# A decoder layer on one core: the bias of the attention's values moves from VectorE's add to a product of TensorE, and ScalarE copies the values out

## The chip, the cores and the metric

The kernel runs on one core of a Trainium2 chip. A core has five engines that run at the same time, each through its own list of instructions in order: TensorE (PE in the profile; its weight loads are PEld), VectorE (DVE), ScalarE (ACT), GpSimd (POOL) and SyncE (SP, which issues most DMAs). They wait for each other through semaphores. The metric is device time in microseconds, a median over runs. Matrix products are written into PSUM, a memory of a few banks that TensorE fills and VectorE or ScalarE reads.

## The reference, cut to what matters

The layer is a Mamba block, a cross attention with a feed-forward part, and a mixture of 160 experts, each with a residual and a layer norm. There are 8 batches of 256 positions, 256 channels wide. The change concerns the line of V:

```
# cross attention; keys = values = ctx, 256 positions a batch
Q = queries @ Wq + bq
K = keys @ Wk + bk
V = values @ Wv + bv
scores = einsum('bqd,bkd->bqk', Q, K) * scale
attn = einsum('bqk,bkd->bqd', softmax(scores), V)
merged = attn @ Wo + bo
x = layer_norm(queries + keys + values + merged, ln1_g, ln1_b)
h = relu(x @ W1 + b1) @ W2 + b2
x = layer_norm(x + h, ln2_g, ln2_b)
# around it: x = layernorm(x + mamba(x)); x = layernorm(x + above); x = layernorm(x + experts(x))
```

## The kernel before, in words

The program has three parts on the time axis: a front (Mamba, attention, feed-forward, router; to about 690 us and a tail to about 765), the experts, and a final combine. The change is in the front.

The front is a software pipeline over the 8 batches. It runs in turns; in turn s the engines work on the state scan of batch s, the attention of batch s-1, the feed-forward of batch s-2, the router of batch s-3 and the projections of batches s+1 and s+2. Each engine has a function `turn(s, p)` that writes out by hand in which order it takes these pieces, so the order on an engine is fixed; p is the parity that picks one of two buffers. An instruction that waits holds up all that its engine has behind it.

The scan of a batch has 16 steps t (4 groups of states for each of 4 chunks of channels). A step goes through four engines: ScalarE writes the decays into a PSUM tile DA (`decay`, L722 and L725: a small copy and four exponentials); GpSimd forms the inflow product (`inflow`, L462); VectorE runs the scan (`scan`, L1662) and multiplies it (`outflow`, L1669); TensorE sums it into the bank Y (`sum_`, L1117). After each four steps VectorE takes the sum out of Y (`y`, L1675 and L1678), and the next first sum of TensorE waits for that.

The keys and values of batch s are made in turn s. TensorE projects the keys into the bank PB (`k_`, L1197), ScalarE copies them out with their bias (L745), TensorE projects the values into the same bank (`v_`, L1206, four products), and VectorE adds the bias row on the way out to the tile vv (`v_`, L1684), between the scan and the outflow of step 12. PB is used next by the projection of batch s+2 (`in_proj`, L1081), which waits for the semaphore v_c that this add raises. Before the first turn that uses them, the weight of V and its row are multiplied by the output projection, so that the row `rows[:, BV, :]` holds the products' bias, the same on all 128 partitions.

The last steps of the feed-forward of batch s-2 stand near by. VectorE adds the residual and takes the moments (`ln2`, L1723, L1688, L1692). GpSimd makes the root (`ln_root`, L468 to L473), then adds an offset for another batch (`x1_offset`, L508). ScalarE normalises (`normalise`, L769), GpSimd multiplies by the norm's weights (`ln2_affine`, L503), and VectorE adds the residual (`ln3`, L1729). On GpSimd, behind L503, follow two scatters of the routed rows of batch s-3 (L515), two more roots, the inflow products of steps 14 and 15 and of the next turn's 0 and 1, the other norm's affine (L491, L493), two scatters, and the product of step 2. On VectorE, in the next turn, the router of batch s-3 forms a mask (`choose`, L1759) behind the outflow of step 0.

On ScalarE the order around the change is: the keys' copy L745, decay 12, decay 13, the normalise L769 of batch s-2, the copy of the projection (`x_in`, L659), decay 14.

Of the kernel before, what the change touches and what calls it, by code (L numbers as in the profile page):

```python
# [11 lines left out]
ALU = mybir.AluOpType  # L12
AX = mybir.AxisListType

P = 128
NB, T, D = 8, 256, 256
NT = NB * T
KD = D // P
QT = T // P
# [61 lines left out]
def decoder_kernel(nc, a, out):  # L81
    ctx = ExitStack()
    with ctx:
        def sb(name, shape, dt=FP32):
            return ctx.enter_context(nc.sbuf_tensor(name, shape, dt))

        def ps(name, shape=(P, 512), dt=FP32):
            return ctx.enter_context(nc.psum_tensor(name, list(shape), dt))

        def sig(name, per=1):  # L90
            return Sig(ctx.enter_context(nc.semaphore(name)), per)
# [22 lines left out]
        w_v = sb("w_v", [P, KD, D])  # L114
# [6 lines left out]
        rows = sb("rows", [P, 7, D])  # L121
        BV, BO, G1, B1, B2, G2, BB2 = range(7)
# [4 lines left out]
        ident = sb("ident", [P, P])  # L127
# [16 lines left out]
        PB = ps("PB")  # L144
# [34 lines left out]
        v_f, v_c, kT_f, kT_c = sig("v_f"), sig("v_c"), sig("kT_f"), sig("kT_c")  # L179
# [4 lines left out]
        vo_f, vo_c = sig("vo_f", 2), sig("vo_c", 2)  # L184
# [29 lines left out]
        ct = sb("ct", [P, KD, T])  # L214
# [19 lines left out]
        vv = sb("vv", [P, QT, D])  # L234
# [43 lines left out]
        def pair(bank):  # L278
            return bank[:, :].rearrange("p (c t) -> p c t", c=2)

        def states(tile):
            return tile[:, :].rearrange("p (n t) -> p n t", n=SG)
# [3 lines left out]
        def exists(b):  # L286
            return not isinstance(b, int) or 0 <= b < NB
# [362 lines left out]
        def front_scalar(act):  # L650
            s = nc.scalar
# [18 lines left out]
            def z_in(b, p, f):  # L670
                if f == 0 and y_d.at(b - 2, NC, True):
                    act.wait_ge(y_d.sem, y_d.at(b - 2, NC))
                act.wait_ge(proj_f.sem, proj_f.at(b, f + 5))
                s.activation(sz[p][:, 2 * f:2 * f + 2, :], pair(PB), ACT.Copy).then_inc(proj_c.sem, 1)
# [38 lines left out]
            def decay(b, p, t):  # L713
                gr, c = t % NG, t // NG
                if t == 0:
                    act.wait_ge(dl_d.sem, dl_d.at(b, 1))
                    if isinstance(b, int) and b == 0:
                        act.wait_ge(k_scaled.sem, 2)
                if outflow_d.at(b, t - NDA + 1, True):
                    act.wait_ge(outflow_d.sem, outflow_d.at(b, t - NDA + 1))  # L720
                da = states(DA[t % NDA])
                s.activation(da[:, :, 0:1], zeros[:, 0:SG].unsqueeze(2), ACT.Copy)  # L722
                for n in range(SG):
                    st = gr * SG + n
                    ins = s.activation(da[:, n, 1:T], dl[p][:, c, 1:T], ACT.Exp, scale=a_neg[:, c, st:st + 1])  # L725
                ins.then_inc(decay_d.sem, 1)
# [74 lines left out]
            for c in range(NC):  # L801
                for k in range(TAPS):
                    ins = s.activation(w_tap[:, c * TAPS + k, :], ident[:, :], ACT.Copy, scale=w_conv[:, c, k:k + 1])
# [35 lines left out]
            def turn(s, p):  # L839
                if exists(s) and s > 0:  # L840
                    decay(s, p, 1)
                    decay(s, p, 2)
                if exists(s + 1) and s >= 0:
                    conv_out(s + 1, 1 - p, 1)
                if exists(s) and s > 0:
                    decay(s, p, 3)
                if exists(s + 1) and s >= 0:
                    z_in(s + 1, 1 - p, 0)
                if exists(s):
                    decay(s, p, 4)  # L850
                if 0 <= s < 3:
                    clear_near(s)
                if exists(s):
                    decay(s, p, 5)
                if exists(s - 2):
                    copy_out(s - 2, x2aT_f, QF, fT, x2aT_c)
                if exists(s - 3):
                    chosen_exp(s - 3)
                if exists(s + 1) and s >= 0:
                    z_in(s + 1, 1 - p, 1)  # L860
                    gates(s + 1, 1 - p)
                if exists(s - 2):
                    ffn1(s - 2, 0)
                if exists(s):
                    decay(s, p, 6)
                if exists(s + 1) and s >= 0:
                    x_proj(s + 1, 1 - p)
                if exists(s - 2):
                    ffn1(s - 2, 1)
                if exists(s):  # L870
                    decay(s, p, 7)
                if s == 0:
                    turned_out()
                if exists(s - 1):
                    normalise(s - 1, 0, x1[1 - p])
                if exists(s - 2):
                    ffn1(s - 2, 2)
                if exists(s - 1):
                    copy_out(s - 1, x1T_f, QA, aT, x1T_c)
                if exists(s):  # L880
                    decay(s, p, 8)
                if s == 2:
                    clear_rest()
                if exists(s + 1) and s >= 0:
                    dt_proj(s + 1, 1 - p, 0)
                if exists(s - 1):
                    q_(s - 1)
                if exists(s - 2):
                    ffn1(s - 2, 3)
                if exists(s):  # L890
                    decay(s, p, 9)
                if s == 0:
                    vo_out()
                if exists(s):
                    decay(s, p, 10)
                if exists(s + 1) and s >= 0:
                    dt_proj(s + 1, 1 - p, 1)
                    softplus(s + 1, 1 - p)
                if exists(s - 1):
                    softmax(s - 1)  # L900
                if exists(s):
                    decay(s, p, 11)
                if exists(s + 1) and s >= 0:
                    softplus_ln(s + 1, 1 - p)
                if exists(s - 1):
                    copy_out(s - 1, pT_f, QA, qT, pT_c)
                if exists(s):
                    k_(s)
                    decay(s, p, 12)
                    decay(s, p, 13)  # L910
                if exists(s - 2):
                    normalise(s - 2, 2, x2[p])
                if exists(s + 2) and s > -2:
                    x_in(s + 2, 0)
                if s == -1:
                    decay(0, 0, 2)
                if exists(s):
                    decay(s, p, 14)
                if exists(s - 2):
                    normalise(s - 2, 3, x2[p])  # L920
                if exists(s + 2) and s > -2:
                    x_in(s + 2, 1)
                if s == -1:
                    decay(0, 0, 3)
                if exists(s - 1):
                    normalise(s - 1, 1, x2a)
                if exists(s):
                    decay(s, p, 15)
                if exists(s - 2):
                    copy_out(s - 2, x2T_f, QF, fT, x2T_c)  # L930
                if exists(s + 1) and s >= 0:
                    decay(s + 1, 1 - p, 0)
                if exists(s + 2) and s > -2:
                    conv_out(s + 2, p, 0)
                if exists(s - 2) and s < L7:
                    shared(s - 2)
                if s == L7:
                    x2aT6_out()
# [125 lines left out]
        def front_tensor(pe):  # L1064
            mm, tr = nc.tensor.matmul, nc.tensor.transpose
# [134 lines left out]
            def v_(b):  # L1200
                pe.wait_ge(kT_c.sem, kT_c.at(b, 1))
                if isinstance(b, int) and b == 0:
                    pe.wait_ge(vo_c.sem, 2)
                for q in range(QT):
                    for k in range(KD):
                        ins = mm(pair(PB)[:, q, :], ct[:, k, q * P:(q + 1) * P], w_v[:, k, :], start=k == 0, stop=k == KD - 1)  # L1206
                ins.then_inc(v_f.sem, 1)

            def x2aT(b):
# [418 lines left out]
        def front_vector(dve):  # L1628
            v = nc.vector
# [47 lines left out]
                dve.wait_ge(y_du.sem, y_du.at(b, c + 1))  # L1677
                v.tensor_tensor(u[p][:, c, :], Y[:, 0:T], sz[p][:, c, :], ALU.mult).then_inc(y_d.sem, 1)  # L1678

            def v_(b):  # L1680
                dve.wait_ge(v_f.sem, v_f.at(b, 1))
                if isinstance(b, int) and b == 0:
                    dve.wait_ge(vo_c.sem, 2)
                v.tensor_tensor(vv[:, :, :], pair(PB), rows[:, BV, :].unsqueeze(1).to_broadcast([P, QT, D]), ALU.add).then_inc(v_c.sem, 1)  # L1684

            def moments(i, src, b):
                for q in range(QT):
                    v.bn_stats(stats[:, i, q, :], src[:, q, :]).then_inc(stat1[i].sem, 1)  # L1688
# [154 lines left out]
            def turn(s, p):  # L1843
# [57 lines left out]
                    ln2(s - 2, p)  # L1901
                if exists(s):
                    scan(s, 12)
                    v_(s)
                    outflow(s, 12)
                if exists(s + 1):
                    delta_u(s + 1, 1 - p)
# [663 lines left out]
```

## Time and profile before

| what | value |
|---|---|
| median of 3 runs | 1117.17 us (1114.88 to 1120.43) |
| the profiled execution | 1118.88 us, span 1117.1 us |
| TensorE busy | 955.9 us (86%) |
| VectorE busy | 849.5 us (76%) |
| GpSimd busy | 746.1 us (67%) |
| ScalarE busy | 626.1 us (56%) |

The profile comes from one execution. Its shares of busy time are means over the three parts; the front alone is read by stretches of time. In the rows further down a time is in microseconds from the span's start, the idle time of the engine ahead of an instruction stands in brackets with what released it, and "L1684" is a line of the kernel. A product of fp32 appears as two records, so "x8" is four products.

### The profile page before, as it was taken

The numbers are of one execution on the slowest core, as the hardware profiler recorded it, in microseconds if no ns is written. First come the engines' busy times: TensorE is split into PE (matmuls) and PEld (weight loads), VectorE is DVE, ScalarE is ACT, GpSimd is POOL, SyncE is SP. The second block draws the span as 40 slices with busy tenths as digits, with TensorE's granted clock in tenths as the row PEclk, the third lists the DMA queues.
The fourth block names the chain that finished last, engine by engine and source line by source line (L and its number), as shares of the span: only waits on it lengthen the run. The fifth ranks groups of instructions, "written<-read, shape, count | busy, mean of one in ns | idle before, by whom it ended". The sixth has DMA issues, their size and how long they took to land. (4 is left out here: it accounts for less than half of the span.)

```text
span 1117.1 us, 17544 instructions
## 1 busy us (share of the span) xinstructions
PE 955.9 (86%) x4878; PEld 800.4 (72%) x4878; DVE 849.5 (76%) x1645; ACT 626.1 (56%) x1555; POOL 746.1 (67%) x648
## 2 busy tenths in 40 slices
PE   6598989999999999999977989824999999999386
PEld 4376767888887887887866867613888778788264
DVE  0669999899999999999999994762655555555276
ACT  4766685775875874875863634412655554555300
POOL 1545575757679879888888986564777777777500
PEclk9698999999999999999998999966999999999789
DMA  7472854825114214214133112437998988988496
GB/s 238 170 258 74 254 170 152 280 84 170 46 47 159 76 64 143 76 69 150 55 98 135 40 45 78 143 113 252 336 294 282 284 289 279 306 273 257 141 371 250
DMA packets 118253, 195.48 MB, mean 175 GB/s; under 512 B 17476, under 2 KB 83170, under 8 KB 115714
## 3 DMA queue, kind: packets, MB, share of 16 engines
q1 hardware_dynamic: 79682, 134.54, 37.1%
q0 software_dynamic: 16512, 35.19, 8.7%
q10 hardware_dynamic: 21952, 24.51, 6.8%
q8 instruction: 43, 0.70, 0.3%
q14 instruction: 64, 0.52, 0.1%
HBM read 155.21 MB, written 75.64 MB: 207 GB/s over the span
## 5 line engine op out<-in xcount | busy, mean ns | idle before, releaser
L462 POOL TENSOR_TENSOR inf_all<-bc_all,du 128x1024 f32<-128x1024 f32 x128 | 300.7, 2366 | 102.6 <-DVEq L1660 53.3
L1662 DVE TENSOR_TENSOR_SCAN DA<-DA,inf_all 128x1024 f32<-128x1024 f32 x128 | 293.1, 2290 | 16.0 <-ACT DA L725 13.2
L2214 POOL DMA_INDIRECT yp_dram<-u,sz x216 | 212.8, 985 | 78.6 <-issue 42.0
L1117 PE MATMUL Y<-hb_all,ident 128*128 128x256 f32 x1024 | 244.6, 386 | 21.8 <-DVE u L1678 20.4
L1117 PEld LDWEIGHTS Y<-hb_all,ident 128*128 128x128 f32 x1024 | 195.0, 193 | 54.0 <-DVE u L1678 24.6
L725 ACT ACTIVATE DA<-dl,a_neg 128x255 f32<-128x255 f32 x512 | 211.9, 461 | 0.2
L2281 ACT ACTIVATE u<-DA,sz 128x256 f32<-128x256 f32 x216 | 102.4, 474 | 117.8 <-DMA yp_dram<-u,sz 91.2
L1669 DVE TENSOR_TENSOR hb_all<-DA,bc_all 128x1024 f32<-128x1024 f32 x128 | 155.9, 1218 | 7.9 <-DVE DA L1662 0.5
L2249 PE MATMUL DA<-hb_all,sz 128*128 128x256 f32 x432 | 137.1, 399 | 20.4 <-ACT sz L2274 18.0
L2242 PE MATMUL DA<-sz,hb_all 128*128 128x128 f32 x864 | 133.2, 277 | 4.0 <-issue 4.0
L2242 PEld LDWEIGHTS DA<-sz,hb_all 128*128 128x128 f32 x864 | 114.9, 194 | 4.5 <-issue 4.4
L2381 DVE COPY sz<-QA 128x256 f32<-128x256 f32 x108 | 45.8, 424 | 88.1 <-PE QA L2233 86.1
L515 POOL DMA_INDIRECT xe_dram<-x2e,ad_i x80 | 85.2, 1065 | 18.2 <-issue 16.7
L722 ACT ACTIVATE DA<-zeros 128x4 f32<-128x4 f32 x128 | 22.4, 175 | 119.5 <-DVE hb_all L1669 116.6
L2249 PEld LDWEIGHTS DA<-hb_all,sz 128*128 128x128 f32 x432 | 66.1, 193 | 29.6 <-ACT sz L2274 26.1
L2274 ACT ACTIVATE sz<-DA 128x128 f32<-128x128 f32 x216 | 58.9, 273 | 34.2 <-PE DA L2242 21.6
L1081 PE MATMUL PB<-xt,w_in 128*128 128x256 f32 x224 | 57.5, 402 | 16.8 <-DMA xt<-in_xT 11.1
L2233 PE MATMUL PB<-ident,inf_all 128*128 128x128 f32 x216 | 42.0, 277 | 33.9 <-DMA inf_all<-xe_dram 33.9
L2381 DVE COPY sz<-PB 128x256 f32<-128x256 f32 x108 | 45.8, 424 | 26.1 <-PE PB L2233 25.1
L1081 PEld LDWEIGHTS PB<-xt,w_in 128*128 128x128 f32 x224 | 43.9, 200 | 27.1 <-DMA xt<-in_xT 11.5
L2233 PEld LDWEIGHTS PB<-ident,inf_all 128*128 128x128 f32 x216 | 30.9, 143 | 45.1 <-DMA inf_all<-xe_dram 34.3
L1090 PE MATMUL PB<-xin,w_tap 128*128 128x256 f32 x224 | 51.1, 380 | 2.5 <-ACT du L667 1.8
(459 smaller groups left out, 1603.7 us busy)
## 6 DMA issues: line engine op xcount, KB each, us to landing
hb_all<-in_w_moe SPq DMA_DIRECT2D x216, 256.0 KB
bc_all<-bc_dram SPq DMA_DIRECT2D x32, 1024.0 KB, 5.8
inf_all<-xe_dram SPq DMA_DIRECT2D x216, 140.0 KB
bc_all<-yp_dram SPq DMA_DIRECT2D x16, 1024.0 KB, 6.6
xe_dram<-zeros ACTq DMA_DIRECT2D x2, 7420.0 KB, 26.0
xe_dram<-zeros ACTq DMA_DIRECT2D x1, 7560.0 KB, 27.1
yp_dram<-u,sz POOLq DMA_INDIRECT x216
xt<-in_xT SPq DMA_DIRECT2D x8, 256.0 KB, 6.1
```

The source lines that it names most:

```text
L462: g.tensor_tensor(inf[(b * NTAU + t) % NI][:, :, :], bc[gr][:, 0, :, :], du[p][:, c, :].unsqueeze(1).to_broadcast([P, SG, T]), ALU.mult).t ...
L515: g.indirect_dma_start(xe_dram, bass.IndirectOffsetOnAxis(ap=ad_i[b % 2][:, q, k:k + 1], axis=0), x2e[p][:, q, :].bitcast(I32), None).then ...
L725: ins = s.activation(da[:, n, 1:T], dl[p][:, c, 1:T], ACT.Exp, scale=a_neg[:, c, st:st + 1])
L1081: ins = mm(pair(PB)[:, i, :], w_in[:, k, c * P:(c + 1) * P], xt[:, k, :], start=k == 0, stop=k == KD - 1)
L1117: ins = mm(Y[:, 0:T], ident[:, :], hb[t % NH][:, n, :], start=gr == 0 and n == 0, stop=gr == NG - 1 and n == SG - 1, skip_group_check=True)
L1662: v.tensor_tensor_scan(da[:, :], da[:, :], inf[(b * NTAU + t) % NI][:, :, :].rearrange("p n t -> p (n t)"), 0.0, ALU.mult, ALU.add).then_i ...
L1669: v.tensor_tensor(hb[t % NH][:, :, :], states(DA[t % NDA]), bc[t % NG][:, 1, :, :], ALU.mult).then_inc(outflow_d.sem, 1)
L2214: g.indirect_dma_start(yp_dram, bass.IndirectOffsetOnAxis(ap=pid[:, half * UNROLL + s_:half * UNROLL + s_ + 1], axis=0), ys[s_][:, :], Non ...
L2242: ins = mm(UP[s_ % 2][:, 0:P], wt[s_][:, k * INTER:(k + 1) * INTER], xgT[s_ % 2][:, k, :], start=k == 0, stop=k == KD - 1)
L2249: mm(DN[s_ % 2][:, 0:D], h1[s_ % 2][:, :], wt[s_][:, KD * INTER:], start=True, stop=True).then_inc(dn_f.sem, 1)
L2281: s.activation(ys[s_][:, :], DN[s_ % 2][:, 0:D], ACT.Identity, scale=both[:, s_, 0:1]).then_inc(dn_c.sem, 1)
L2381: v.tensor_copy(xgT[s_ % 2][:, :, :], XT[s_ % 2][:, 0:KD * P].rearrange("p (k t) -> p k t", k=KD)).then_inc(xgT_c.sem, 1)
```

## The change

The values' bias is added while the products are summed: for each half q of the positions TensorE first multiplies the identity matrix `ident` by the row `rows[:, BV, :]` into PB, and the two products of the values are summed on top. The copy out of PB to vv, and the raising of v_c, move from VectorE to ScalarE (`copy_out`, L728 to L730). VectorE's `v_` is gone.

```
                 if exists(s):
                     k_(s)
                     decay(s, p, 12)
+                    copy_out(s, v_f, PB, vv, v_c)
                     decay(s, p, 13)
...
                 for q in range(QT):
+                    mm(pair(PB)[:, q, :], ident[:, :], rows[:, BV, :], start=True, stop=False)
                     for k in range(KD):
-                        ins = mm(pair(PB)[:, q, :], ct[:, k, q * P:(q + 1) * P], w_v[:, k, :], start=k == 0, stop=k == KD - 1)
+                        ins = mm(pair(PB)[:, q, :], ct[:, k, q * P:(q + 1) * P], w_v[:, k, :], start=False, stop=k == KD - 1)
                 ins.then_inc(v_f.sem, 1)
...
-            def v_(b):
-                dve.wait_ge(v_f.sem, v_f.at(b, 1))
-                if isinstance(b, int) and b == 0:
-                    dve.wait_ge(vo_c.sem, 2)
-                v.tensor_tensor(vv[:, :, :], pair(PB), rows[:, BV, :].unsqueeze(1).to_broadcast([P, QT, D]), ALU.add).then_inc(v_c.sem, 1)
...
                 if exists(s):
                     scan(s, 12)
-                    v_(s)
                     outflow(s, 12)
```

The function that the copy calls was there already:

```
            def copy_out(b, filled, bank, dst, done):
                act.wait_ge(filled.sem, filled.at(b, 1))
                s.activation(dst[:, :, :], pair(bank), ACT.Copy).then_inc(done.sem, 1)
```

On ScalarE, in turn 4, from the keys' copy to the copy of the projection, before:

```order
L745 ACTIVATE kT<-PB,b_k 128x256 x2
L722 ACTIVATE DA<-zeros 128x4
L725 ACT_TABLE_LOAD
L725 ACTIVATE DA<-dl,a_neg 128x255 x4
L722 ACTIVATE DA<-zeros 128x4
L725 ACTIVATE DA<-dl,a_neg 128x255 x4
L769 ACTIVATE x2e<-x2e,off,rs 128x256 x2
L659 ACTIVATE xin<-PB 128x2x256
```

The same place now (kT and vv are the keys and values, DA the decays, x2e the rows of batch s-2, xin the projection of batch s+2):

```order
L745 ACTIVATE kT<-PB,b_k 128x256 x2
L722 ACTIVATE DA<-zeros 128x4
L725 ACT_TABLE_LOAD
L725 ACTIVATE DA<-dl,a_neg 128x255 x4
L730 ACTIVATE vv<-PB 128x512
L722 ACTIVATE DA<-zeros 128x4
L725 ACTIVATE DA<-dl,a_neg 128x255 x4
L769 ACTIVATE x2e<-x2e,off,rs 128x256 x2
L659 ACTIVATE xin<-PB 128x2x256
```

The copy of vv stands ahead of decay 13 and of the normalise L769. On TensorE, in turn 4, from the sum of step 8 (Y) and the attention's products (QA) to the next projection, before:

```order
L1117 MATMUL Y<-hb_all,ident 128x256 x4
L1166 MATMUL QA<-vv,qT 128x256 x4
L1206 MATMUL PB<-w_v,ct 128x256 x4
L1117 MATMUL Y<-hb_all,ident 128x256 x8
L1081 MATMUL PB<-xt,w_in 128x256 x4
```

The same place now (lines behind the edit count one more):

```order
L1118 MATMUL Y<-hb_all,ident 128x256 x4
L1167 MATMUL QA<-vv,qT 128x256 x4
L1206 MATMUL PB<-rows,ident 128x256
L1208 MATMUL PB<-w_v,ct 128x256 x2
L1206 MATMUL PB<-rows,ident 128x256
L1208 MATMUL PB<-w_v,ct 128x256 x2
L1118 MATMUL Y<-hb_all,ident 128x256 x8
L1082 MATMUL PB<-xt,w_in 128x256 x4
```

Two products more stand ahead of the sums of steps 9 and 10.

## Rows read from the trace of the kernel before

**Rows 1.** Windows: busy time of each engine in three stretches, granted clock, DMA.
```profile
core 0: us, PE busy (x) PEld busy (x) DVE busy (x) ACT busy (x) POOL busy (x), PEclk, DMA share, GB/s
378.00:459.00 81.00, 78.71 (x370) 66.15 (x369) 78.77 (x97) 57.21 (x136) 67.49 (x55) 1.00 0.29 96
408.88:434.90 26.02, 25.44 (x120) 21.41 (x119) 24.98 (x34) 14.25 (x37) 24.02 (x22) 1.00 0.62 210
356.30:360.00 3.70, 3.64 (x12) 3.04 (x13) 3.60 (x4) 2.28 (x6) 2.65 (x2) 0.70 0.00 0
```
**Rows 2.** Timeline of VectorE, the mask: start, duration, instruction, idle before, releaser.
```profile
513.65 2.92 DVE L1759 TENSOR_SCALAR msk_b<-rep 128x320 bf16<-128x320 f32 x1
...
731.49 0.33 DVE L1759 TENSOR_SCALAR msk_b<-rep 128x320 bf16<-128x320 f32 x1
```
**Rows 3.** Timeline of GpSimd beside the first of those masks.
```profile
513.05 0.96 POOL L515 DMA_INDIRECT xe_dram<-x2e,ad_i  x1 [0.30 <-issue]
514.02 2.36 POOL L462 TENSOR_TENSOR inf_all<-bc_all,du 128x1024 f32<-128x1024 f32 x1
```
**Rows 4.** Timeline of GpSimd in turn 4.
```profile
407.63 1.27 POOL L508 TENSOR_TENSOR x<-x,rows 128x512 f32<-128x512 f32 x1
408.88 1.27 POOL L503 TENSOR_TENSOR x2e<-x2e,rows 128x512 f32<-128x512 f32 x1
```
**Rows 5.** Timeline of ScalarE in turn 4.
```profile
404.40 1.65 ACT L725 ACTIVATE DA<-dl,a_neg 128x255 f32<-128x255 f32 x4
407.71 1.09 ACT L769 ACTIVATE x2e<-x2e,off,rs 128x256 f32<-128x256 f32 x2 [1.66 <-POOL off L473]
412.55 0.60 ACT L659 ACTIVATE xin<-PB 128x512 f32<-128x512 f32 x1 [3.75 <-PE PB L1081]
...
413.13 1.65 ACT L725 ACTIVATE DA<-dl,a_neg 128x255 f32<-128x255 f32 x4
```
**Rows 6.** Timeline of VectorE in turn 4.
```profile
405.81 2.30 DVE L1662 TENSOR_TENSOR_SCAN DA<-DA,inf_all 128x1024 f32<-128x1024 f32 x1
408.02 0.67 DVE L1684 TENSOR_TENSOR vv<-PB,rows 128x512 f32<-128x512 f32 x1
408.61 1.21 DVE L1669 TENSOR_TENSOR hb_all<-DA,bc_all 128x1024 f32<-128x1024 f32 x1
...
411.15 0.68 DVE L1729 TENSOR_TENSOR x2e<-x2e,x 128x512 f32<-128x512 f32 x1
...
416.25 2.29 DVE L1662 TENSOR_TENSOR_SCAN DA<-DA,inf_all 128x1024 f32<-128x1024 f32 x1
418.65 1.23 DVE L1669 TENSOR_TENSOR hb_all<-DA,bc_all 128x1024 f32<-128x1024 f32 x1
```
**Rows 7.** Timeline of TensorE in turn 4.
```profile
405.44 1.89 PE L1206 MATMUL PB<-w_v,ct 128*128 128x256 f32 x8
407.17 3.62 PE L1117 MATMUL Y<-hb_all,ident 128*128 128x256 f32 x16
```
**Rows 8.** Timeline of VectorE, the third y of turns 0 and 1.
```profile
106.02 0.49 DVE L1675 SCALAR_TENSOR_TENSOR Y<-u,d_par,Y 128x256 f32<-128x256 f32 x1 [1.70 <-PE Y L1117]
...
177.62 0.49 DVE L1675 SCALAR_TENSOR_TENSOR Y<-u,d_par,Y 128x256 f32<-128x256 f32 x1 [1.24 <-PE Y L1117]
```
**Rows 9.** Timeline of TensorE in turn 0, the projection behind the values.
```profile
102.20 1.97 PE L1081 MATMUL PB<-xt,w_in 128*128 128x256 f32 x8 [0.31 <-DVE vv L1684]
```
**Rows 10.** Timeline of TensorE, the values of turns 2, 3 and 7.
```profile
244.64 1.67 PE L1206 MATMUL PB<-w_v,ct 128*128 128x256 f32 x7
...
322.61 1.89 PE L1206 MATMUL PB<-w_v,ct 128*128 128x256 f32 x8
...
645.80 1.89 PE L1206 MATMUL PB<-w_v,ct 128*128 128x256 f32 x8
```
**Rows 11.** Timeline of GpSimd, L503 of turns 3 and 7.
```profile
327.02 1.27 POOL L503 TENSOR_TENSOR x2e<-x2e,rows 128x512 f32<-128x512 f32 x1
...
649.37 1.27 POOL L503 TENSOR_TENSOR x2e<-x2e,rows 128x512 f32<-128x512 f32 x1
```
**Rows 12.** Timeline of VectorE, the residual add L1729 of turn 2.
```profile
250.10 0.68 DVE L1729 TENSOR_TENSOR x2e<-x2e,x 128x512 f32<-128x512 f32 x1
```

More of the change, by code:

```diff
@@ L909, in turn @@
                     decay(s, p, 12)
+                    copy_out(s, v_f, PB, vv, v_c)
                     decay(s, p, 13)
@@ L1204, in v_ @@
                 for q in range(QT):
+                    mm(pair(PB)[:, q, :], ident[:, :], rows[:, BV, :], start=True, stop=False)
                     for k in range(KD):
-                        ins = mm(pair(PB)[:, q, :], ct[:, k, q * P:(q + 1) * P], w_v[:, k, :], start=k == 0, stop=k == KD - 1)
+                        ins = mm(pair(PB)[:, q, :], ct[:, k, q * P:(q + 1) * P], w_v[:, k, :], start=False, stop=k == KD - 1)
                 ins.then_inc(v_f.sem, 1)
@@ L1678, in y @@
                 v.tensor_tensor(u[p][:, c, :], Y[:, 0:T], sz[p][:, c, :], ALU.mult).then_inc(y_d.sem, 1)
[L1680 to L1684, printed above, removed]
             def moments(i, src, b):
@@ L1903, in turn @@
                     scan(s, 12)
-                    v_(s)
                     outflow(s, 12)
```

## The prediction, made before the changed kernel was run

> **What bounds the kernel now.** I read the busy time by stage first, then the timeline of each engine through one turn of the front's loop (turn 4, from 378 to 459 us), then the same few lines in the other turns. The edit runs once in each of the eight turns, all of which lie in the front (up to about 690 us), so nothing after the front matters unless the front ends later or earlier.
>
> In turn 4 VectorE is busy 78.77 of 81 us and TensorE 78.71, ScalarE 57.21 [rows 1]. That reads as "VectorE is the bound", and the removed add stands on it. The reader is to see two things that correct this. First, a part of VectorE's busy time is a wait. The mask of the router (L1759) takes 2.92 us in one turn and 0.33 us in the tail, and the long one ends 0.19 us after GpSimd's product that began at 514.02 [rows 2, 3]. So in the turns that route, VectorE does not pass the mask before GpSimd has finished the inflow product of step 2. Second, GpSimd has no room ahead of that product: between the affine step of the feed-forward's norm (L503, at 408.88) and the end of that product in the next turn it is busy 24.02 of 26.02 us with 22 instructions [rows 1], the rest being the gaps between them. So when L503 starts late, the decay-scan loop of VectorE starts its next turn late by about as much. L503 in turn 4 began when GpSimd had finished the step before it in its own order (L508, 407.63 + 1.27 = 408.90), and the values that it multiplies were ready at 407.71 + 1.09 = 408.80, from ScalarE's normalise L769 [rows 4, 5]. The two are a tenth apart: L769 is already as late as L503 can bear.
>
> **The change part by part.** *Removed from VectorE:* one add of 128x512 per turn. In turn 4 the scan starts at 405.81 and its outflow at 408.61, with the add between; without an add a scan at 416.25 is followed by its outflow at 418.65. So it is worth 2.80 - 2.40 = 0.40 us per turn, not its own 0.67 [rows 6]. In turns 3 to 6 that gain sits in the stretch that GpSimd's chain covers, in turns 0 and 1 ahead of a wait for TensorE; I book 0, and keep 8 x 0.40 = 3.2 us as the other end.
>
> *Added to TensorE:* two products of ident with the row per turn. Four products of the same shape take 407.17 - 405.44 = 1.73 us [rows 7], so two cost 0.87 us, and the values' bank is full 0.87 us later. In turns 0 and 1 the end of TensorE's later sum is what VectorE waits for (1.70 and 1.24 us before y) [rows 8]. In turn 1 all 0.87 appear. In turn 0 TensorE itself had waited 0.31 us for the removed add [rows 9]; that wait goes, since the copy is done while the two sums run: 0.56. (If turn 1's products run at the lower clock, 1.7.)
>
> *Added to ScalarE, with a wait:* the copy, between the decays of steps 12 and 13. Its nearest row is a copy of 128x512 out of the same bank, 0.60 us; the next instruction but one, the exponentials of a decay, starts 0.58 after the copy's start and runs 1.65 [rows 5]. Before, the exponentials of decay 13 ran at 404.40 and L769 waited behind it for GpSimd's root until 407.71. Now the copy stops ScalarE's order until TensorE has filled the bank, and decay 13 and L769 are queued behind it. That ScalarE holds ready work behind a waiting instruction is in the rows: the copy L659 sat 3.75 us until 412.55 with the next decay behind it, whose outflow had been ready since 408.61 + 1.21 = 409.82 [rows 5, 6]. (The Trainium skill, "TensorE: Matmul & The Clock Gate", section "Architectural detail: the array is 16x 32x32, not 1x 128x128", calls ScalarE's queue a strict FIFO; the row agrees. Were it not so, the sum would be the price of TensorE's products alone, about 1.4 us.)
>
> So L503 starts at: end of the old four products + 0.87 (two more) + 0.05 (hand-over, an estimate) + 0.58 + 1.65 (copy and decay 13) + 1.09 (L769) + 0.05 = end + 4.29. Turn by turn:
> - Turn 4: products end 405.44 + 1.89 = 407.33, L503 at 411.62 in place of 408.88: +2.74 [rows 4, 7].
> - Turn 3: 322.61 + 1.89 = 324.50, L503 at 328.79 in place of 327.02: +1.77 [rows 10, 11]. Turns 5 and 6 have the same spacing; three such turns: 5.31.
> - Turn 7: 645.80 + 1.89 = 647.69, L503 at 651.98 in place of 649.37: +2.61 [rows 10, 11].
> - Turn 2 has no scatters to fill GpSimd, so there only the consumer counts: L503 ends at 246.31 + 4.29 + 1.27, and VectorE's residual add (L1729) starts at 251.92 in place of 250.10: +1.82 [rows 10, 12]. (The bank is full at 244.64 + 1.67 = 246.31.)
>
> In turn 4 VectorE would itself stop before L1729: 411.62 + 1.27 + 0.05 = 412.94 in place of 411.15 [rows 6]. VectorE, TensorE and GpSimd meet again in every turn (TensorE waits for y before its first sum), so each turn's loss is carried and nothing gives it back; the experts start on the front's end.
>
> Sum: 0.56 + 0.87 + 1.82 + 5.31 + 2.74 + 2.61 = 13.9 us. The profiled execution took 1118.88 us (span 1117.1), 1.71 above the median of 1117.17; the changed kernel would be 1132.8 by that execution, and 1131.1 as a median.
>
> The ends of what no row shows: the two hand-overs at 0 or at 0.2 each give -0.6 or +1.8 over six turns. GpSimd's 2.0 us of gaps [rows 1] are between its own instructions; were half of them to close under the delay, four routing turns would give 4 us back. With VectorE's 3.2 on top the low end is 13.9 - 0.6 - 4.0 - 3.2 = 6.1, 1123.3; I take the sum without these, as the rows of L503 are its nearest. The upper end is the clock's, below.
>
> **The rivals.**
> *Relief decides.* VectorE is the busiest of the elementwise engines, so it takes its 0.40 us in each turn: 1117.2 - 3.2 = 1114.0, not slower. It holds if the bank is full early enough that L769 is still released by GpSimd's root: the six products would have to end 3.42 us before L503's old start, in turn 3 by 327.02 - 3.42 = 323.60; they end at 324.50 + 0.87 = 325.37, 1.8 too late [rows 10, 11]. Against it. (The Trainium skill, "Perfetto Trace Analysis", section "Optimizing Scalar/DVE Operations", advises to hand work to ScalarE where VectorE is saturated; by that rule the kernel gains. The mask's rows speak against the saturation that it presumes.)
>
> *The mask slips in first.* After the change GpSimd is later against VectorE by some tenths, so the mask might run before the product instead of behind it: 2.92 - 0.33 = 2.6 us back in up to four turns, 1131.1 - 10.4 = 1120.7 at the most, about 1126 for two turns. For it: the start order is close. Against: at 513.65 the mask began 0.37 us ahead of the product and still waited, as a scatter of GpSimd ran up to it [rows 2, 3]. (The Trainium skill, "SBUF — State Buffer", section "SBUF: two separate sides", says that VectorE and GpSimd take one port pair as an exclusive lock, whoever starts first; in these rows the one that started later by the records won.)
>
> *The clock falls more often.* TensorE now waits longer for VectorE in each turn. In turn 4, after it had waited for y, the granted clock was 0.70 from 356.3 to 360 us [rows 1], between the levels of 1.2 and 2.4 GHz, and its later products came about 1 us later against VectorE than in turn 3 (407.33 is 1.52 after the scan's start [rows 6, 7], and L503 loses 2.74 there and not 1.77). If turns 5 and 6 go the same way, each costs 1 to 2 us more: 1134.
>
> *Only TensorE's price.* The blocked queue turns out to be hidden, and TensorE is the bound in all turns: 8 x 0.87 = 7.0, 1124.1. Against it: in the rows of turns 2, 3, 4 and 7 the way through ScalarE and L503 costs 1.8 to 2.7, so TensorE's 0.87 is not what ends last [rows 4, 7, 10, 11].
>
> **How the numbers follow.** My forecast has 0.62 (12 to 16 us, 1129 to 1133); the falling clock 0.12; the mask 0.10; TensorE alone 0.07; relief 0.09. About 0.5% (5.6 us) is what a measurement of this kernel can tell from no change. Slower than that: the first two, nearly all of the mask's cases below two and a half turns, and half of TensorE alone, 0.62 + 0.12 + 0.06 + 0.04 = 0.84. Faster than 0.5% would need more than the relief's whole 3.2 us, 0.03; the rest, 0.13, is within. The range leaves out the relief and the far end of the mask below, and more than two extra falls of the clock above: 1122 to 1137.
>
> **What would show it.** Right: ScalarE idle before the copy of vv, released by TensorE's PB, some 3.5 us in turn 4; L769 of turns 2 to 7 no longer released by GpSimd's root but run directly behind decay 13; L503 about 1.8 us later after the scan of step 12, 2.7 in turn 4; a new idle time of VectorE before L1729, some 1 to 2 us, released by L503; the mask still long, turns longer by 1.7 to 2.7 us, turns 0 and 1 by less than 1. Wrong: L769 still waiting for the root, no idle time before L1729, or a mask of 0.3 to 0.7 us in turns 4 to 7; wrong altogether if the turns keep their length.

## The result, and the profile after

The changed kernel takes 1128.93 us (median of 10 runs, 1122.14 to 1132.25), before beside it 1116.72 (10 runs, 1114.68 to 1120.43): 12.2 us more, ratio 1.0103 with a 95% interval of 1.0082 to 1.0124. A second set of runs gave 1131.44 against 1116.83: 1.0115 (1.0074 to 1.0156). The profiled execution took 1129.65 us, its span 1127.9 (before: 1118.88 and 1117.1).

VectorE is busy 846.0 us instead of 849.5, TensorE 963.6 instead of 955.9: both moved as the edit says, by little. The waits tell more. These are rows of the view of waits of the changed kernel (engine, name and line that waited, releaser: us in total, times, longest):

```profile
ACT vv L730 <- PE PB L1208: 23.7, 7, 5.2
...
ACT x2e L769 <- POOL off L473: 15.1, 6, 4.3
...
POOL x2e L503 <- ACT x2e L769: 11.2, 6, 2.7
...
DVE x2e L1725 <- POOL x2e L503: 10.0, 6, 2.8
...
DVE DA L1664 <- POOL inf_all L462: 3.8, 5, 2.6
```

The first row is new: ScalarE's copy waits 23.7 us for TensorE's bank, once in each of turns 1 to 7. The third and fourth are what it leads to, six times each, once in each of turns 2 to 7. The second has shrunk, from 11 waits to 6: in turns 2 to 7 the L769 ahead of L503 no longer waits for GpSimd's root. The same row before:

```profile
ACT x2e L769 <- POOL off L473: 21.6, 11, 3.5
```

(VectorE's residual add is L1725 now, L1729 before; its scan L1664, L1662 before.)

The timeline of ScalarE in turn 4 of the changed kernel, against [rows 5]:

```profile
409.77 0.60 ACT L730 ACTIVATE vv<-PB 128x512 f32<-128x512 f32 x1 [3.43 <-PE PB L1208]
410.27 0.17 ACT L722 ACTIVATE DA<-zeros 128x4 f32<-128x4 f32 x1
410.36 1.66 ACT L725 ACTIVATE DA<-dl,a_neg 128x255 f32<-128x255 f32 x4
411.96 1.08 ACT L769 ACTIVATE x2e<-x2e,off,rs 128x256 f32<-128x256 f32 x2
414.95 0.60 ACT L659 ACTIVATE xin<-PB 128x512 f32<-128x512 f32 x1 [1.92 <-PE PB L1082]
```

In [rows 5] L769 had 1.66 us of idle time in front of it, released by GpSimd's root. Here it has none: it runs directly behind decay 13, and decay 13 behind the copy. TensorE's side, against [rows 7]:

```profile
406.98 0.59 PE L1206 MATMUL PB<-rows,ident 128*128 128x256 f32 x2
407.41 1.03 PE L1208 MATMUL PB<-w_v,ct 128*128 128x256 f32 x4
408.28 0.59 PE L1206 MATMUL PB<-rows,ident 128*128 128x256 f32 x2
408.71 1.03 PE L1208 MATMUL PB<-w_v,ct 128*128 128x256 f32 x4
```

The bank is full at 408.71 + 1.03 = 409.74, and the copy starts 0.03 us later.

Turn 3 shows how far the delay goes. GpSimd and VectorE of the changed kernel there (scan 12 starts at 325.84; before, at 323.93):

```profile
330.65 1.26 POOL L503 TENSOR_TENSOR x2e<-x2e,rows 128x512 f32<-128x512 f32 x1 [1.70 <-ACT x2e L769]
332.08 1.51 POOL L515 DMA_INDIRECT xe_dram<-x2e,ad_i  x1 [0.17 <-issue]
...
338.16 2.36 POOL L462 TENSOR_TENSOR inf_all<-bc_all,du 128x1024 f32<-128x1024 f32 x1
```

```profile
325.84 2.30 DVE L1664 TENSOR_TENSOR_SCAN DA<-DA,inf_all 128x1024 f32<-128x1024 f32 x1
...
329.39 1.22 DVE L1657 TENSOR_TENSOR du<-dl,u 128x1024 f32<-128x1024 f32 x1
331.94 0.69 DVE L1725 TENSOR_TENSOR x2e<-x2e,x 128x512 f32<-128x512 f32 x1 [1.34 <-POOL x2e L503]
...
336.71 2.29 DVE L1664 TENSOR_TENSOR_SCAN DA<-DA,inf_all 128x1024 f32<-128x1024 f32 x1
...
340.65 2.30 DVE L1664 TENSOR_TENSOR_SCAN DA<-DA,inf_all 128x1024 f32<-128x1024 f32 x1 [0.32 <-POOL inf_all L462]
```

The same stretch before, where the prediction had not shown it, first GpSimd, then VectorE:

```profile
328.45 1.87 POOL L515 DMA_INDIRECT xe_dram<-x2e,ad_i  x1 [0.17 <-issue]
...
335.02 2.36 POOL L462 TENSOR_TENSOR inf_all<-bc_all,du 128x1024 f32<-128x1024 f32 x1
```

```profile
323.93 2.30 DVE L1662 TENSOR_TENSOR_SCAN DA<-DA,inf_all 128x1024 f32<-128x1024 f32 x1
...
327.86 1.51 DVE L1655 TENSOR_TENSOR du<-dl,u 128x1024 f32<-128x1024 f32 x1
329.29 0.68 DVE L1729 TENSOR_TENSOR x2e<-x2e,x 128x512 f32<-128x512 f32 x1
...
337.58 2.29 DVE L1662 TENSOR_TENSOR_SCAN DA<-DA,inf_all 128x1024 f32<-128x1024 f32 x1
```

Measured from scan 12, L503 [rows 11] moved from 3.09 to 4.81 us, +1.72. VectorE's residual add moved from 5.36 to 6.10, +0.74 only; the inflow product of step 14 from 11.09 to 12.32, +1.23; scan 14, which now waits 0.32 us for that product, +1.16 (from 13.65 to 14.81). Scan 4 of the next turn, the mark that is used for a turn's end below, comes 1.18 later. So two thirds of L503's delay arrive.

The mask of the changed kernel, against [rows 2], one row for each of turns 4 to 7 and one of the tail:

```profile
353.56 2.80 DVE L1755 TENSOR_SCALAR msk_b<-rep 128x320 bf16<-128x320 f32 x1
...
436.03 2.79 DVE L1755 TENSOR_SCALAR msk_b<-rep 128x320 bf16<-128x320 f32 x1
...
518.48 2.82 DVE L1755 TENSOR_SCALAR msk_b<-rep 128x320 bf16<-128x320 f32 x1
...
600.95 2.79 DVE L1755 TENSOR_SCALAR msk_b<-rep 128x320 bf16<-128x320 f32 x1
...
738.82 0.33 DVE L1755 TENSOR_SCALAR msk_b<-rep 128x320 bf16<-128x320 f32 x1
```

It is as long as it was. The last scan of the front (step 15 of turn 7) starts at 670.84 us, before at 662.91. So 7.9 of the 10.8 us by which these two profiled executions differ lie in the front.

### The profile page after: what moved, and what is told of

Same layout as the page of the kernel before. It is cut to its first block and busy times, and to the rows that moved or that the text cites. A ratio compares the mean times of both kernels' runs of the same rounds, so it can differ in the third digit from the quotient of the medians.

```text
span 1127.9 us, 17607 instructions
## 1 busy us (share of the span) xinstructions
PE 963.6 (85%) x4910; PEld 806.8 (72%) x4910; DVE 846.0 (75%) x1637; ACT 628.8 (56%) x1563; POOL 745.4 (66%) x648
## 5 line engine op out<-in xcount | busy, mean ns | idle before, releaser
L1664 DVE TENSOR_TENSOR_SCAN DA<-DA,inf_all 128x1024 f32<-128x1024 f32 x128 | 293.2, 2290 | 18.4 <-ACT DA L725 14.6
L1118 PE MATMUL Y<-hb_all,ident 128*128 128x256 f32 x1024 | 245.4, 387 | 24.0 <-DVE u L1680 23.7
```

The source lines that it names most:

```text
L1118: ins = mm(Y[:, 0:T], ident[:, :], hb[t % NH][:, n, :], start=gr == 0 and n == 0, stop=gr == NG - 1 and n == SG - 1, skip_group_check=True)
L1664: v.tensor_tensor_scan(da[:, :], da[:, :], inf[(b * NTAU + t) % NI][:, :, :].rearrange("p n t -> p (n t)"), 0.0, ALU.mult, ALU.add).then_i ...
```

## The experiments

All times are medians, each beside runs of before on the same chip in the same set: 1116.72 us for the first pair, and 1115.82, 1116.83 and 1117.04 in three later sets, each on a chip of its own. Kernels of different sets are therefore compared by their ratios to before, and a difference "by the ratios" is one in ratio times 1117 us. "Last scan" and "combine" come from the one profiled execution of each row; "combine" is the stretch from its first product to the end of the span.

| kernel | us | ratio to before, 95% interval | last scan | combine |
|---|---|---|---|---|
| before, two profiles | 1115.8 to 1117.0 | 1 | 662.91, 657.48 | 55.1, 52.7 |
| changed, two profiles | 1128.93, 1131.44 | 1.0103 (1.0082-1.0124), 1.0115 (1.0074-1.0156) | 670.84, 671.43 | 58.5, 56.6 |
| copy last | 1117.53 | 1.0020 (0.9995-1.0045) | 666.01 | 58.6 |
| VectorE copies | 1121.16 | 1.0045 (1.0016-1.0075) | 664.15 | 52.7 |
| VectorE copies, ScalarE waits | 1123.99 | 1.0080 (1.0052-1.0109) | 670.36 | 53.1 |
| changed, no bias | 1122.08 | 1.0049 (1.0025-1.0072) | 668.11 | 57.1 |
| copy last, no bias | 1117.03 | 0.9995 (0.9973-1.0017) | 658.24 | 56.6 |
| copy last, bias in base | 1120.18 | 1.0027 (1.0004-1.0050) | 667.18 | 52.7 |
| before, mask first | 1106.53 | 0.9909 (0.9887-0.9930) | 652.07 | 52.2 |
| changed, mask first | 1116.23 | 0.9987 (0.9968-1.0005) | 662.43 | 52.4 |
| copy last, mask first | 1106.22 | 0.9912 (0.9888-0.9935) | 654.57 | 52.1 |
| bias in base, mask first | 1112.14 | 0.9952 (0.9933-0.9970) | 656.35 | 53.6 |

### Is it the copy's place on ScalarE, TensorE's products, or something behind the front?

**Copy last.** The copy goes behind decay 13 and L769; nothing else differs from the changed kernel.

```
                     decay(s, p, 12)
-                    copy_out(s, v_f, PB, vv, v_c)
                     decay(s, p, 13)
                 if exists(s - 2):
                     normalise(s - 2, 2, x2[p])
+                if exists(s):
+                    copy_out(s, v_f, PB, vv, v_c)
```

> ScalarE's copy of the values stands behind decay 13 and behind the normalise L769; TensorE's two bias products stay. Theory (the copy's wait for TensorE's bank holds decay 13 and L769): L769 is released by GpSimd's root again, GpSimd's L503 and VectorE's residual add keep their old distance from scan 12, the turns are as long as before: 1114 to 1119 us, ratio 0.997 to 1.002. Rival A (only TensorE's two products cost): the products are still there, 1124 us or more, 1.006. Rival B (the loss of the front is about 7 us, the rest of the 12 comes behind it, in experts or combine, and belongs to the changed program whatever ScalarE does): front as before, total 1120 to 1122.

1117.53 us, ratio 1.0020: some 9 to 11 us of the loss are gone by the ratios, with TensorE's two products still there. L769 is released by GpSimd's root again (21.2 us in 11 waits), as this row of its waits shows. No wait of L503 for L769 is left, and of the residual add for L503 one of 0.7 us in turn 7, where before has one of 0.4:

```profile
ACT x2e L769 <- POOL off L473: 21.2, 11, 3.9
```

The theory stands; rival A falls as the whole cause. (The profile is of an execution of 1125.1 us, 7.6 over this kernel's median, so its last scan and its combine in the table are not those of a usual run.)

**VectorE copies.** TensorE adds the bias, VectorE copies PB in the place of its old add; ScalarE's call of `copy_out` is taken out, so that its list is that of before.

```
+            def v_(b):
+                dve.wait_ge(v_f.sem, v_f.at(b, 1))
+                v.tensor_copy(vv[:, :, :], pair(PB)).then_inc(v_c.sem, 1)
...
                     scan(s, 12)
+                    v_(s)
                     outflow(s, 12)
```

> TensorE adds the bias with its two products, but VectorE copies the bank out in the old place; ScalarE's list is that of before. It isolates TensorE's price. Theory: 1117 to 1119 us, ratio 1.000 to 1.002 (up to 0.87 us in each of turns 0 and 1, the other turns hide it). Rival A: 8 x 0.87 = 7.0 us, 1124. Rival B: 1120 to 1122.

1121.16, ratio 1.0045 (1.0016 to 1.0075): 5.0 us over before (1.8 to 8.4), between the theory's 2 at the most and rival A's 7.0, both of which lie in the interval. In its profile scan 13 of turn 1 comes 0.86 us later behind scan 12 than before and that of turn 2 0.2; from scan 12 to scan 4 of the next turn, turns 3 and 4 keep their length within 0.1. Its last scan is 1.2 us later than in the first profile of before and 6.7 later than in the second, so one profile doesn't settle the price. What the products cost without the stall lies, by the medians, between nothing (copy last with the mask first, below) and these 5 us.

**VectorE copies, ScalarE waits.** The same, with the wait alone put back.

```
                     decay(s, p, 12)
+                    act.wait_ge(v_f.sem, v_f.at(s, 1))
                     decay(s, p, 13)
```

> As the kernel where VectorE copies, and ScalarE gets the wait for TensorE's bank between decays 12 and 13, without a copy. It isolates the stall. Theory: decay 13 and L769 come late as in the changed kernel, less the copy's 0.58 us; L503 later by 1 to 2 us a turn; 5 to 8 us more than without the wait, 1123 to 1127. Rival A: no change against the kernel without the wait. Rival C (the copying itself costs, by ScalarE's time or by the bank's release through ScalarE, not the wait): no change either.

The ratio rises from 1.0045 to 1.0080, 3.9 us, a little under the expected 5 to 8; the two intervals overlap, so the times alone would not settle it. The profiles do: the last scan comes 6.2 us later, and the chain is back. No copy runs on ScalarE here, so rival C falls: the wait does it. L503 of turn 3 starts 4.32 us after scan 12 (worked out: 3.09 + 1.77 - 0.58 = 4.28), and all three steps of the chain are in its waits:

```profile
ACT DA L722 <- PE PB L1208: 26.9, 8, 4.7
...
ACT x2e L769 <- POOL off L473: 15.2, 6, 5.1
...
POOL x2e L503 <- ACT x2e L769: 8.9, 6, 2.2
...
DVE x2e L1729 <- POOL x2e L503: 7.3, 6, 1.4
```

**Changed, no bias.** The two products go, and with them the bias, which this kernel leaves out; ScalarE's copy stays where the change put it.

```
-                    mm(pair(PB)[:, q, :], ident[:, :], rows[:, BV, :], start=True, stop=False)
                     for k in range(KD):
-                        ins = mm(pair(PB)[:, q, :], ct[:, k, q * P:(q + 1) * P], w_v[:, k, :], start=False, stop=k == KD - 1)
+                        ins = mm(pair(PB)[:, q, :], ct[:, k, q * P:(q + 1) * P], w_v[:, k, :], start=k == 0, stop=k == KD - 1)
```

> The changed kernel without the two bias products, so the bias of the values is left out; ScalarE's copy stays where it is. Theory: the bank is full 0.87 us earlier, so L503 is too, in turns 2 to 7, and most of the stall stays: by the working 13.9 - 6 x 0.87 - 1.43 = 7.3 us over before, by two thirds of it as the traces measured, 4 to 5 us: 1121 to 1125. Rival A (TensorE's products are the whole cost): 1114 to 1117, as before or a little under it.

1122.08, 1.0049: 5.5 us over before without any product more on TensorE. By the ratios 6 to 7 us have come back, as much as was worked out (6 x 0.87 + 1.43 = 6.65); in the profiled front only 2.7 and 3.3 (668.11 against 670.84 and 671.43). The rows show why it is less there. GpSimd's L503 of turn 3 starts 0.86 us earlier after scan 12 than in the changed kernel (3.95), but takes 1.95 us, since it begins while VectorE's du (325.97 to 327.19) runs; VectorE's residual add gains 0.17 us (5.93 for 6.10). In turns 5 and 6 the add is even later than in the changed kernel's first profile (6.19 for 5.95 and 6.02), since the bank was full later (1.51 us after scan 12 for 1.28 and 1.34): TensorE's granted clock had fallen there, to 0.57 and 0.68 in the 4 us that begin 12 us behind scan 0, and was 1.00 in the other. Turn 3, first GpSimd, then VectorE:

```profile
326.37 1.95 POOL L503 TENSOR_TENSOR x2e<-x2e,rows 128x512 f32<-128x512 f32 x1 [0.84 <-ACT x2e L769]
```

```profile
325.97 1.22 DVE L1656 TENSOR_TENSOR du<-dl,u 128x1024 f32<-128x1024 f32 x1
328.35 0.69 DVE L1724 TENSOR_TENSOR x2e<-x2e,x 128x512 f32<-128x512 f32 x1 [1.16 <-POOL x2e L503]
```

### Second profiles, and what VectorE's relief is worth

**The changed kernel and before again**, unchanged.

> The changed kernel once more, for a second profile: the last scan came 7.9 us later than before in the first pair of profiles, the medians lie 12.2 us apart. Theory (the loss is the front's, about 8 us, and the rest is what executions differ by): last scan 5 to 9 us after that of before (662.9), the combine's length anywhere between 52 and 59 us, median 1123 to 1128. Rival B (the changed program has a longer combine too): the stretch from the combine's first product to the end is 58 us or more again, where before had 55.1, and the median is 12 us over before again.

> The kernel before once more, one look, for a second profile. Theory: last scan within 2 us of 662.9 (the clock's falls in turns 0, 1 and 4 come and go), combine anywhere between 52 and 59 us. Rival B: combine 55 us or less.

The changed kernel's front comes out alike (671.43 us for the last scan), but its median of 1131.44 is above the 1123 to 1128 of the theory. The front of before does not come out alike: 657.48 in place of 662.91, and not within 2 us of it; its one execution took 1110.93 us. Of these 5.4 us, 1.5 are there ahead of the place of the edit in turn 0, 1.35 arise in turn 1, and 2.07 at one mask: in turn 5 VectorE's mask took 0.33 us, because GpSimd was about 1 us later (it had waited 0.99 us for a DMA) and VectorE got in first. These are the four masks of turns 4 to 7 in the second profile of before:

```profile
347.51 2.84 DVE L1759 TENSOR_SCALAR msk_b<-rep 128x320 bf16<-128x320 f32 x1
...
429.31 0.33 DVE L1759 TENSOR_SCALAR msk_b<-rep 128x320 bf16<-128x320 f32 x1
...
508.27 2.77 DVE L1759 TENSOR_SCALAR msk_b<-rep 128x320 bf16<-128x320 f32 x1
...
589.64 2.74 DVE L1759 TENSOR_SCALAR msk_b<-rep 128x320 bf16<-128x320 f32 x1
```

The combine is 52.1 to 58.6 us over all kernels. Without the stall it was 58.6 and 56.6, with it 53.1 and 52.4, so it does not go with the stall, and rival B is not shown. It is not excluded either: of the kernels without the mask first, five of the six profiles in which ScalarE copies the values have 56.6 us or more, and the four in which VectorE does have 55.1 or less. The sixth (bias in base, 52.7) and the kernels with the mask first (52.1 to 53.6) don't fit that, and no run tests it.

**Copy last, no bias.** VectorE's relief, with ScalarE's copy behind L769 as its only price: the kernel with the copy last, less the two products of TensorE (the edit of "changed, no bias"), so the bias is left out.

> VectorE's add is gone, ScalarE copies behind L769, and TensorE has no bias products: the bias of the values is left out. It isolates VectorE's relief. Theory (GpSimd's chain covers turns 3 to 6, so VectorE's 0.40 us shows only in turns 0, 1, 2 and 7): 0 to 1.6 us under before, ratio 0.9985 to 1.000. Rival D (VectorE's relief is worth its 0.40 us in all turns): 3.2 us under, 0.997 or less.

0.9995 (0.9973 to 1.0017): nothing that can be told from before. Rival D's 3.2 us would be 0.9971, just outside. With this kernel the four cases are complete, in us over before by the ratios: neither products nor stall -0.6, products alone (copy last) 2.2, stall alone (changed, no bias) 5.5, both 11.5 and 12.8. So by the medians the products cost more where the stall is, as they make ScalarE wait longer; with intervals of more than 2 us either way on each, that excess of 3 to 4.5 us is not clear of noise.

**Copy last, bias in base.** The bias is added by GpSimd, one more add of 128x512 a turn.

```
-                g.tensor_tensor(x2a[:, :, :], x2a[:, :, :], x2a[:, :, :], ALU.add).then_inc(base_d.sem, 1)
+                g.tensor_tensor(x2a[:, :, :], x2a[:, :, :], x2a[:, :, :], ALU.add).then_inc(base_v.sem, 1)
+                pool.wait_ge(base_v.sem, base_v.at(b, 1))
...
+                g.tensor_tensor(x2a[:, :, :], x2a[:, :, :], row(BV), ALU.add).then_inc(base_d.sem, 1)
```

> As the kernel with the copy last and no bias products, but the bias is not left out: the weights of a softmax row sum to 1 once divided, so the row is added to the base that the attention's output is added to, by GpSimd, one add of 128x512 (1.27 us) a turn behind L482, ahead of a stretch in which GpSimd waits 4.8 us. Theory: hidden there, time within 1 us of the kernel without the bias, 0 to 1.6 us under before (0.9985 to 1.000). Rival E (GpSimd's list is full in that place too): 1.27 us in each of five or more turns, 6 us over, 1.005.

1120.18, 3.0 us over before by the ratio (0.4 to 5.6): not the theory's 0 to 1.6 under, and half of rival E's 6. The theory's cover was looked for in the wrong place: GpSimd's idle time (4.8 us in turn 4 of before) comes behind the inflow products, and VectorE now has an idle 1.10 us ahead of scan 10 in turn 5, where before has none. That scan's inflow product starts 6.11 us after scan 8 in place of 4.76.

### Does the stall reach the turn's end through the mask?

**Mask first**, on four kernels: before, changed, copy last, and copy last with the bias in the base. GpSimd starts the inflow product of step 2 only when VectorE's mask is done:

```
                     scatter(s - 4, p, 8)
+                if exists(s) and exists(s - 3):
+                    pool.wait_ge(mask_d.sem, mask_d.at(s - 3, 1))
                 if exists(s):
                     inflow(s, p, 2)
```

> The kernel before, with one wait more: GpSimd starts the inflow product of step 2 only when VectorE's mask of the same turn is done, so the mask can't be caught behind it. In one mask of the second profile of before that happened by itself (mask 0.33 in place of 2.4 us, the next scan 2.07 us earlier). Theory (the long mask is a wait, and the turn's end waits with it): four masks of 0.3 to 0.5 us, 4 x 2.1 to 2.5 = 8 to 10 us under before, 1106 to 1109, ratio 0.991 to 0.993. Rival F (GpSimd's chain is the bound: the product is then late for scan 2, or TensorE for the next sums): 0 to 3 us under before.

> The changed kernel with the same wait. Theory as predicted (the stall reaches VectorE through GpSimd's chain and the mask): with the mask ahead of the product the stall of turns 3 to 6 has no way to the turn's end, and the kernel comes within 6 us of before with the mask first. Rival G (VectorE is held by L503 itself and by the inflow of step 14, ahead of the mask): the full 12 to 14 us remain between the two, that is about 1120.

> TensorE adds the bias, ScalarE copies behind L769, and the mask is first. Without the copy's stall and with the mask's wait gone VectorE's list is what is left: Theory (VectorE's 0.40 us a turn counts where GpSimd no longer ends the turn, TensorE's products cost 1 to 3 us in all): 2 us under to 2 us over before with the mask first. Rival A (TensorE's products are then the bound): 4 to 7 us over it.

> The bias added by GpSimd to the attention's base, ScalarE copies behind L769, no bias products on TensorE, and the mask is first. Theory (VectorE's list is the bound): 1 to 3 us under before with the mask first. Rival E (GpSimd's extra add is in the way): 2 to 5 us over it.

*Before, mask first:* 1106.53, ratio 0.9909: 10 us faster than before, the fastest kernel here with the copy-last one. GpSimd and VectorE in turn 5:

```profile
428.29 2.35 POOL L462 TENSOR_TENSOR inf_all<-bc_all,du 128x1024 f32<-128x1024 f32 x1 [0.65 <-DVE msk_b L1761]
```

```profile
427.75 0.33 DVE L1761 TENSOR_SCALAR msk_b<-rep 128x320 bf16<-128x320 f32 x1
427.99 2.29 DVE L1664 TENSOR_TENSOR_SCAN DA<-DA,inf_all 128x1024 f32<-128x1024 f32 x1
```

GpSimd gives up 0.65 us, and scan 1 comes 5.34 us after scan 0 in place of 7.42 in the first profile of before, 2.1 us earlier. Over turns 4 to 7 this comes to some 9 us. The long mask was a wait, as [rows 2, 3] had been read; it could be taken away by itself, and rival F falls.

*Changed, mask first:* 1116.23. By the ratios it gains 13 to 14 us, and it stays 9.7 us over before with the mask first. That is between the theory's 6 and rival G's 12 to 14, nearer to G. The masks are 0.33 to 0.38 us long and wait for nothing, so the stall has another way: VectorE waits for L503 itself (10.6 us in six waits; 10.0 in six without the mask first).

```profile
POOL x2e L503 <- ACT x2e L771: 11.8, 6, 2.7
...
DVE x2e L1727 <- POOL x2e L503: 10.6, 6, 3.1
```

This pair is also the cleanest: the last scans lie 10.4 us apart (662.43, 652.07), the combines 0.2, the medians 9.7. Of the 10.4 us, 7.3 arise in turns 2 to 7 behind scan 12 (table below) and 2.6 in turns 0 and 1, 2.2 of them at scan 13 of turn 1, which can come at either of two levels in any kernel (below).

*Copy last, mask first:* 1106.22, equal to before with the mask first by the medians (0.3 us under). Rival A, 4 to 7 us over, falls here: TensorE's products are not the bound even with the mask's wait gone. *Bias in base, mask first:* 1112.14, 5.6 and 5.9 us slower than these two by the medians; the theory's 1 to 3 us under is missed, and it is a little more than rival E's 2 to 5.

## Why the prediction was right, and where its terms were not

**The bound.** Right that VectorE's 97% is not work alone: the mask's 2.8 us are a wait behind GpSimd, worth 10 us in all. Wrong in what it was used for. The prediction let the whole delay of L503 pass through GpSimd's list to the mask. VectorE is held earlier, by its residual add of L503's own output and by the inflow of step 14; with the mask made short, the loss stays 9.7 us, and turns 3 to 5 lose 0.8 to 1.2 us each as they do with the long mask (0.9 to 1.2 in the first pair).

**ScalarE's copy holds decay 13 and L769.** Right, and shown from two sides: the wait alone brings the stall back, the copy moved behind L769 takes 9 to 11 us of the loss away. (The Trainium skill, "TensorE: Matmul & The Clock Gate", section "Architectural detail: the array is 16x 32x32, not 1x 128x128", calls ScalarE's queue a strict FIFO. Copy last against the changed kernel agrees: the place in the list alone is worth some 9 to 11 us by the ratios.)

**The sizes.** From scan 12 of a turn to scan 4 of the next (turn 7: to scan 14), in us over before. "First pair" and "changed again" are both against the first profile of before; against the second, turn 4 would show 2.1 us more, the mask that slipped in:

| turn | predicted | first pair | changed again | mask-first pair |
|---|---|---|---|---|
| 2 | 1.82 | 1.76 | 1.88 | 1.75 |
| 3 | 1.77 | 1.18 | 1.17 | 1.16 |
| 4 | 2.74 | 1.06 | 2.18 | 0.76 |
| 5 | 1.77 | 0.92 | 0.92 | 1.13 |
| 6 | 1.77 | 1.16 | 2.18 | 0.11 |
| 7 | 2.61 | 2.06 | 2.45 | 2.39 |

Turn 2 is as worked out, and turn 7 to about 0.2 us but for the first pair, where it loses 0.55 less. In turns 3, 5 and 6 L503 is late by 1.59 to 1.72 us in the first pair, close to the "+1.77" of the sum. The step that failed is the one from there to the turn's end, "starts its next turn late by about as much": before, VectorE had reached its add 1.00 us behind the end of L503 (329.29 against 327.02 + 1.27), so that much of the delay is covered there, and on GpSimd's way the first scatter took 1.51 in place of 1.87 us. The prediction worked out VectorE's own stop for turn 4 (1.79, [rows 6]), took GpSimd's 2.74 all the same, and only turn 2 was priced by the consumer. (0.11 in the last column: there turn 6 of before with the mask first was itself 1.05 us longer than in copy last with the mask first, 39.25 for 38.20.)

Turn 4's 2.74 rested on a fall of TensorE's clock. Windows of the changed kernel's two profiles around it, first the one without a fall, then the one with (columns as in [rows 1]; the second pair of windows begins 0.45 us later in its turn):

```profile
356.47:360.47 4.00, 1.96 (x13) 1.51 (x12) 3.96 (x5) 0.00 (x0) 3.97 (x3) 1.00 0.09 36
360.47:364.47 4.00, 4.00 (x20) 3.54 (x19) 3.90 (x4) 2.65 (x8) 2.93 (x2) 1.00 0.00 0
```

```profile
353.98:357.98 4.00, 1.96 (x10) 1.55 (x9) 3.96 (x5) 0.36 (x2) 3.98 (x3) 0.86 0.10 36
357.98:361.98 4.00, 4.00 (x15) 3.26 (x15) 3.90 (x3) 2.74 (x8) 2.92 (x2) 0.72 0.00 0
```

With the clock at 1.00 the bank was full 1.27 us after scan 12, with the fall 2.37, and L503 was late by 1.57 and 2.67. Turn 6 differs in the same way (bank 1.34 and 2.37; granted clock 1.00 and 0.57 in the 4 us that begin 12 us behind scan 0). So the rival "the clock falls more often" is an event of single turns, worth 1.0 to 1.1 us each. In the kernel before it fell in turn 4 of the first profile and not of the second, and L503 started 3.07 us after scan 12 in both: there L503 did not hang on the bank, and now it does.

**Turns 0 and 1**, +1.43 predicted: from scan 12 to scan 13 turn 1 takes 8.06 or 9.41 us before and 8.58 or 10.27 in the changed kernel; the difference of the two levels is 0.52 and 0.86 (predicted 0.87), but which level comes is worth more than that. Turn 0 takes 7.70 and 7.69 us before and 6.16 in both profiles of the changed kernel: 1.5 us less, where 0.56 more was predicted. TensorE's granted clock from scan 8 to scan 12 was 0.82 in both of before, 1.00 and 0.91 in the changed kernel's. In the mask-first pair it was 0.82 in both, and there turn 0 takes 7.69 and 8.08, 0.39 more. So the term is right within 0.2 us at one clock, and the clock outweighs it.

**The rivals.** Relief and "only TensorE's price" fell. The mask did not slip in first in any of the changed kernel's eight masks.

**VectorE's relief**, booked at 0: right as far as can be measured, 0.9995 (copy last, no bias).

**The sum.** 13.9 was predicted, the two sets gave 12.2 and 14.6, but the turns above add up to 8.1 and 10.8 against 12.5. Turns 0 and 1, from scan 12 of turn 0 to scan 12 of turn 2, did not add 1.4 to that in these two but took off 2.4 and 2.3. So the total is nearer than its terms, which is luck: terms that were too large met a loss outside of the sum. The four pairings of a front of the changed kernel with one of before differ by 7.9 to 14.0 us, 10.9 on average. In before a mask slipped in first once in eight, for 2.07 us, and that is within these 10.9. What remains, some 2 to 3 us, stays open: the combine of the changed kernel's two profiles is longer too (58.5 and 56.6 for 55.1 and 52.7), but not by anything that the runs tie to the edit.

## What to carry to other kernels

An instruction given to an engine with idle time brings its wait along: ask what stands behind it in that engine's list, and put it behind the work that is due before its operand arrives. Price a delay by the first consumer that it reaches, less that consumer's own room, and not by the whole list of the engine in between. Where a short instruction shows a long busy time beside another engine's, try to order the two: one semaphore wait gave 10 us here, nearly what the change cost.

## What the runs showed of the hardware

In these rows VectorE's and GpSimd's elementwise products shut each other out, and whoever is later pays as busy time, not as idle time: L503 takes 1.26 us when it starts after VectorE's du (330.65 against 329.39 + 1.22) and 1.95 when it starts 0.40 us after du's start; du takes 1.22 us alone and 1.51 when it starts 0.43 us ahead of the end of L503. In both, the later one ends as if it had begun at the other's end, within 0.15 us. (The Trainium skill, "SBUF — State Buffer", section "SBUF: two separate sides", calls the shared port pair an exclusive lock; these rows agree.)

TensorE waited 2.04 us for VectorE in turn 4, behind the same products and 10.98 us after scan 0, in both profiles of the changed kernel. In one its granted clock then had a mean of 0.72 over the window shown, between its levels of 1.2 and 2.4 GHz, and in the other it stayed at 1.00: the fall is not fixed by the program's order alone.
